# Row maxima turned by VectorE block transposes, and one PSUM bank for the projections

## The reference

```python
xq = jnp.einsum('btd,hrd->bthr', x, Q)
xk = jnp.einsum('bud,hrd->buhr', x, K)
scores = jnp.einsum('bthr,buhr->bthu', xq, xk) / sqrt(dim)
attn = jax.nn.softmax(scores, axis=3)
return jnp.einsum('bthu,bud,hde->bte', attn, x, VO)
```

```python
x = x + 0.5 * _L0_ffn_ref(_layernorm(x, axis=-1), ...)
x = x + _L0_attn_ref(_layernorm(x, axis=-1), ...)
x = x + 0.5 * _L0_ffn_ref(_layernorm(x, axis=-1), ...)
```

## Time and profile before

| | us |
|---|---|
| median of 3 runs | 1075.48 |
| the 3 runs | 1075.07 to 1076.77 |
| the profiled execution, its own time | 1076.03 |
| its span in the trace | 1074.2 |

### The profile page before, as it was taken

One profiled execution on the slowest core, in us unless ns is written; L12 is line 12 of the kernel. 1 busy time (PEld: TensorE's weight loads), 2 busy tenths in 40 slices (PEclk: granted clock), 3 DMA queues, 4 the chain that ended last, 5 costly groups with the idle time before them and its releaser, 6 DMA issues.

```text
span 1074.2 us, 21731 instructions
## 1 busy us (share of the span) xinstructions
PE 989.8 (92%) x6145; PEld 514.2 (48%) x6145; DVE 802.9 (75%) x1335; ACT 802.0 (75%) x1294; POOL 785.2 (73%) x707
## 2 busy tenths in 40 slices
PE   4758569999999999999999999999999999996897
PEld 3646324444444444444444444444444444444664
DVE  7545897777777777777777777777777777778455
ACT  4638368888887788887788888778888778885763
POOL 2624338888888888888888888888888888894442
PEclk9879889999999999999999999999999999998899
DMA  9000021222222222222222222222222222210002
GB/s 233 1 1 1 19 70 46 66 64 61 59 59 59 59 59 59 62 63 64 62 63 64 61 59 59 59 59 59 59 62 63 64 63 62 65 34 1 1 1 79
DMA packets 71675, 59.02 MB, mean 55 GB/s; under 512 B 11168, under 2 KB 70560, under 8 KB 71648
## 3 DMA queue, kind: packets, MB, share of 16 engines
q1 hardware_dynamic: 71392, 58.31, 22.1%
q10 hardware_dynamic: 256, 0.39, 0.1%
HBM read 6.23 MB, written 2.10 MB: 8 GB/s over the span
## 4 chain that ended last, share of the span: by engine, by line
PE 76%; DVE 13%; POOL 6%; issue 4%; ACT 1%; DMA 1%; SPq 0%; DVEq 0%; POOLq 0%; ACTq 0%
PE ps L995 11%; PE ps L996 10%; PE ps L997 10%; PE ps L985 10%; PE ps L986 10%; PE ps L972 6%; PE ps L1008 3%; PE ps L964 3%; PE ps L1007 3%; PE ps L1009 3%; DVE work_b L701 3%; PE ps L966 2%; PE ps L965 2%; DVE hT L708 2%; POOL u_u L332 1%
## 5 line engine op out<-in xcount | busy, mean ns | idle before, releaser
L373 POOL TENSOR_TENSOR p_lo<-work_b,p_hi 128x1024 f16<-128x1024 f32 x256 | 539.6, 2129 | 148.1 <-ACT p_hi L525 148.1
L779 DVE TENSOR_REDUCE mcol<-ps 128x2 f16<-128x1024 f32 x256 | 301.7, 1223 | 41.1 <-PE ps L972 41.0
L520 ACT ACTIVATE work_b<-ps,exp_scale 128x1024 f32<-128x1024 f32 x256 | 271.4, 1111 | 38.6 <-PE ps L986 38.4
L525 ACT ACTIVATE p_hi<-work_b 128x1024 f16<-128x1024 f32 x256 | 256.0, 1054 | 0.0
L985 PE MATMUL ps<-head_ops 128*128 128x512 f16 x512 | 195.0, 381 | 3.8 <-DVE mcol L779 2.4
L995 PE MATMUL ps<-p_hi,xn_hi 128*128 128x512 f16 x512 | 195.7, 382 | 0.0
L986 PE MATMUL ps<-head_ops 128*128 128x512 f16 x512 | 195.1, 381 | 0.0
L996 PE MATMUL ps<-p_hi,xn_lo 128*128 128x512 f16 x512 | 195.0, 381 | 0.0
L997 PE MATMUL ps<-p_lo,xn_hi 128*128 128x512 f16 x512 | 194.8, 380 | 0.0
L379 POOL TENSOR_TENSOR x<-x,o_sb 128x512 f32 (+1 forms) x128 | 162.8, 1272 | 10.6 <-DVE o_sb L798 10.6
L530 ACT ACTIVATE y_hi<-ps 128x512 f16<-128x512 f32 x128 | 76.4, 597 | 117.0 <-PE ps L997 116.8
(11 more groups left out here) (113 smaller groups left out, 1412.0 us busy)
## 6 DMA issues: line engine op xcount, KB each, us to landing
head_ops<-pair_ops SPq DMA_DIRECT2D x512, 64.0 KB, 2.0
head_ops<-pair_ops SPq DMA_DIRECT2D x128, 128.0 KB, 2.4
x<-x_dram SPq DMA_DIRECT2D x8, 256.0 KB, 6.1
out<-x SPq DMA_DIRECT2D x8, 256.0 KB, 3.0
vo_last<-wvo_dram SPq DMA_DIRECT2D x1, 1024.0 KB, 13.2
qk<-wq_dram SPq DMA_DIRECT2D x1, 512.0 KB, 5.4
qk<-wk_dram SPq DMA_DIRECT2D x1, 512.0 KB, 6.2
scl<-scales_dram ACTq DMA_DIRECT2D x8, 48.0 KB, 5.4
```

The lines of the kernel that those rows point to most:

```text
L373: pool.tensor_tensor(p_lo[:, par, rows, :], p32[:, par, rows, :], p_hi[:, par, rows, :], ALU.subtract).then_inc(plo_done, 1)
L520: nc.scalar.activation(p32[:, par, 2 * a:2 * a + 2, :], s_ps[a], ACT.Exp, scale=exp_scale[:, 0:1]).then_inc(exp_done, 1)
L525: nc.scalar.activation(p_hi[:, par, 2 * a:2 * a + 2, :], p32[:, par, 2 * a:2 * a + 2, :], ACT.Copy).then_inc(phi_done, 1)
L779: nc.vector.tensor_reduce(mcol[:, par, t, M_ROWS], s_ps[t % 2], AX.X, ALU.max, negate=True).then_inc(max_red, 1)
```

## The change

The turn of the maxima leaves TensorE. `mcol` becomes 32 columns wide for each of two heads and four tiles, the reduction writes column 0 of each 32-wide block, and VectorE turns the blocks of 32x32 itself, with four transposes of 32 partitions each, straight into `q2`. `turn_max`, its identity and its semaphore go.

Keys and queries of a pair are projected in two different slots, keys in the even slot six ahead and queries in the odd slot five ahead, both into bank 5. `q_low` and `k_low` are put behind `y_low` in VectorE's order. The written-out slots begin at -6 instead of -5. `outputs` now waits for the high half of y before its first two matmuls and for the low half before the third.

```diff
-        mcol = sb("mcol", [128, 2, TT, 128], F16)
-        M_ROWS = slice(R, R + 64, 32)
+        mcol = sb("mcol", [128, 2, 2, TT, 32], F16)
+        M_ROW = slice(R, R + 32)
...
-        qj_ps = ps[:, 5, :]
-        kj_ps = ps[:, 7, :]
+        pj_ps = ps[:, 5, :]
...
-            pool.memset(head_ops[64:65, 0:RING:2, 3, :], 1.0).then_inc(prep_p, 1)
-            pool.memset(head_ops[96:97, 1:RING:2, 3, :], 1.0).then_inc(prep_p, 1)
+            pool.memset(head_ops[64:65, 0:2, 3, :], 1.0).then_inc(prep_p, 1)
+            pool.memset(head_ops[64:65, 2:RING, 3, :], 1.0).then_inc(prep_p, 1)
...
(ScalarE's slot)
-                if j % 2 == 1 and hi + 5 < NH:
-                    ...
-                    q_high(pair, ((j + 5) // 2) % 2)
-                    k_high(pair, ((j + 5) // 2) % 2)
+                ahead = 6 - j % 2
+                if hi + ahead < NH:
+                    pair = 2 * turn + (j + ahead) // 2
+                    if lo + ahead >= 4:
+                        pair_free(pair, ((j + ahead) // 2) % 2, turn + (j + ahead) // 4)
+                    if j % 2 == 0:
+                        k_high(pair, ((j + ahead) // 2) % 2)
+                    else:
+                        q_high(pair, ((j + ahead) // 2) % 2)
...
(VectorE)
-                nc.vector.tensor_reduce(mcol[:, par, t, M_ROWS], s_ps[t % 2], AX.X, ALU.max,
+                nc.vector.tensor_reduce(mcol[:, par, :, t, 0], s_ps[t % 2], AX.X, ALU.max,
                                         negate=True).then_inc(max_red, 1)
 
-            def row_max(pair, ring):
-                dve.wait_ge(m_turned, pair + 1)
-                rows = qj_ps[64:128, :].rearrange("p (a t) -> p a t", a=1).to_broadcast([64, 2, T])
-                nc.vector.tensor_copy(q2[64:128, ring:ring + 2, :], rows).then_inc(m_ready, 1)
+            def row_max(mine, k, pair, par, ring):
+                if not isinstance(k, int) or k >= 2:
+                    dve.wait_ge(s_done, 2 * k)
+                dve.wait_ge(max_red, 4 * pair + 4)
+                for q in range(4):
+                    rows = q2[M_ROW, ring:ring + 2, :].rearrange("p a (t c) -> p a t c", c=128)
+                    ins = nc.vector.transpose(rows[:, :, :, 32 * q:32 * q + 32], mcol[32 * q:32 * q + 32, par, :, :, :])
+                ins.then_inc(m_ready, 1)
...
(TensorE)
-                if j % 2 == 0 and lo >= -2 and hi + 2 < NH:
-                    pe.wait_ge(max_red, 2 * k + 8)
-                    pe.wait_ge(ql_ready, projected(i, j))
-                    turn_max(k + 2, (j // 2 + 1) % 2)
                 if lo >= 1:
-                    pe.wait_ge(yl_ready, k)
+                    pe.wait_ge(yh_ready, k)
                     if lo >= 2:
                         pe.wait_ge(o_scaled, k - 1)
-                    pe.wait_ge(kl_ready, projected(i, j))
...
+                    if t == 0:
+                        pe.wait_ge(yl_ready, k)
                     ins = nc.tensor.matmul(o, y_lo[:, cols], vh, start=False, stop=True)
...
-                    project(qj_ps, 0, pj_head * R, quads // QPB, q_proj)
-                    if lo >= 1:
-                        pe.wait_ge(o_scaled, k)
-                    project(kj_ps, 1, pj_head * R, quads // QPB, k_proj)
+                    if j % 2 == 0:
+                        if lo >= -4:
+                            pe.wait_ge(ql_ready, pair)
+                        project(pj_ps, 1, pj_head * R, quads // QPB, k_proj)
+                    else:
+                        pe.wait_ge(kl_ready, pair + 1)
+                        project(pj_ps, 0, pj_head * R, quads // QPB, q_proj)
```

More of the change, by code:

```diff
@@ L314, in _ @@
             pool.memset(xn_lo[:, :, D - 1:D], 0.0).then_inc(prep_p, 1)
-            pool.memset(mcol[:, :, :, :], 0.0).then_inc(prep_p, 1)
+            pool.memset(mcol[:, :, :, :, :], 0.0).then_inc(prep_p, 1)
             pool.wait_ge(prep_p, 4)
@@ L415, in _ @@
             act.wait_ge(consts, 2)
-            nc.scalar.activation(ident_b[:, :], ident[:, :], ACT.Copy)
-            nc.scalar.activation(ident16[:, :], ident[:, :], ACT.Copy).then_inc(prep_a, 1)
+            nc.scalar.activation(ident_b[:, :], ident[:, :], ACT.Copy).then_inc(prep_a, 1)
             def pre(f, s):
@@ L511, in q_high @@
                 act.wait_ge(q_proj, pair + 1)
-                nc.scalar.activation(pair_ops[:, buf, 0, :], qj_ps, ACT.Copy).then_inc(qh_ready, 1)
+                nc.scalar.activation(pair_ops[:, buf, 0, :], pj_ps, ACT.Copy).then_inc(qh_ready, 1)
             def k_high(pair, buf):
                 act.wait_ge(k_proj, pair + 1)
-                nc.scalar.activation(pair_ops[:, buf, 2, :], kj_ps, ACT.Copy).then_inc(kh_ready, 1)
+                nc.scalar.activation(pair_ops[:, buf, 2, :], pj_ps, ACT.Copy).then_inc(kh_ready, 1)
             def exps(k, par, a):
@@ L550, in slot @@
                     p_high(k + 1, (j + 1) % 2, 1)
-                if j % 2 == 1 and hi + 5 < NH:
[L552 to L555, removed]
-                    q_high(pair, ((j + 5) // 2) % 2)
-                    k_high(pair, ((j + 5) // 2) % 2)
+                turn = k // 4 if quad[0] is None else quad[0]
+                ahead = 6 - j % 2
[7 more added lines that the diff above has]
+                        q_high(pair, ((j + ahead) // 2) % 2)
                 if 0 <= lo < SG:
@@ L565, in _ @@
             quad = [None]
-            for k in range(-5, 4):
+            for k in range(-6, 4):
                 slot(k, k % 4, k, k)
@@ L802, in slot @@
                 if j % 2 == 0 and lo >= -2 and hi + 2 < NH:
-                    row_max(2 * i + (j // 2 + 1), (j + 2) % 4)
+                    row_max(mine, k, 2 * i + (j // 2 + 1), (j // 2 + 1) % 2, (j + 2) % 4)
                 if lo >= 1 and lo - 1 < NH:
@@ L810, in slot @@
                         reduce_max(2 * k + (8 + a), (j // 2) % 2, 2 * (j % 2) + a)
[L811 to L818, removed]
                 if 0 <= lo < SG:
@@ L822, in slot @@
                     y_low(k)
-            for k in range(-5, 4):
+                ahead = 6 - j % 2
+                if hi + ahead < NH:
+                    pair = 2 * i + (j + ahead) // 2
+                    buf = ((j + ahead) // 2) % 2
+                    if lo + ahead >= 4:
+                        dve.wait_ge(spread_done[buf][0], 80 * (i + (j + ahead) // 4))
+                        dve.wait_ge(spread_done[buf][1], 80 * (i + (j + ahead) // 4))
+                    if j % 2 == 0:
+                        k_low(pair, buf)
+                    else:
+                        q_low(pair, buf)
+            for k in range(-6, 4):
                 slot(link, k // 4, k, k % 4, k, k)
@@ L974, in maxima @@
                 ins.then_inc(max_mm, 1)
[L976 to L980, removed]
             def scores(k, ring, a):
@@ L999, in weigh, with outputs @@
                     ins.then_inc(av_half, 1)
-            def outputs(head):
+            def outputs(k, head):
                 vh = vo_hi[:, bass.ds(head, 1), 0:RW].rearrange("p a d -> p (a d)")
@@ L1027, in slot @@
                         scores(k + 1, (j + 1) % 4, a)
-                if j % 2 == 0 and lo >= -2 and hi + 2 < NH:
-                    pe.wait_ge(max_red, 2 * k + 8)
-                    pe.wait_ge(ql_ready, projected(i, j))
-                    turn_max(k + 2, (j // 2 + 1) % 2)
                 if lo >= 1:
-                    pe.wait_ge(yl_ready, k)
+                    pe.wait_ge(yh_ready, k)
                     if lo >= 2:
                         pe.wait_ge(o_scaled, k - 1)
-                    pe.wait_ge(kl_ready, projected(i, j))
                     if hi < SG:
                         pe.wait_ge(xsplit_done, SG + k)
-                    outputs((4 * i + (j - 1)) % H)
+                    outputs(k, (4 * i + (j - 1)) % H)
                 if 0 <= lo < NH:
@@ L1056, in slot @@
                     weigh(j % 2, 1, i // QPB)
[L1057 to L1064, removed]
-                    project(qj_ps, 0, pj_head * R, quads // QPB, q_proj)
-                    if lo >= 1:
-                        pe.wait_ge(o_scaled, k)
-                    project(kj_ps, 1, pj_head * R, quads // QPB, k_proj)
+                ahead = 6 - j % 2
+                if hi + ahead < NH:
+                    pair = 2 * i + (j + ahead) // 2
+                    quads = i + (j + ahead) // 4
+                    pj_head = (quads % QPB) * 4 + (j + ahead) % 4
+                    if j % 2 == 0:
+                        if lo >= -4:
+                            pe.wait_ge(ql_ready, pair)
+                        project(pj_ps, 1, pj_head * R, quads // QPB, k_proj)
+                    else:
+                        pe.wait_ge(kl_ready, pair + 1)
+                        project(pj_ps, 0, pj_head * R, quads // QPB, q_proj)
                 if 0 <= lo < SG:
```

7 lines of the change are left out of this document (2 added, 5 removed).

## The result

The changed kernel takes 1069.2 us (median of 11 runs, 1067.2 to 1072.9), against 1075.95 for the kernel before in the same comparison: a ratio of 0.9936 (0.992 to 0.9951). The forecast was 1073.1. The profiled execution took 1072.72 us with a span of 1070.9, so it lies 3.5 above its own median.

A forecast was written before the change was run, and what follows sets the result against it. TensorE was taken as the bound, at 12.93 us a pair of slots. 1076.0 - 4.9 (steady pairs) + 2.0 (start) + 0.5 (end) = 1073.6 for the profiled execution, so 1073.1 for the median, range 1056 to 1087.

The forecast's parts named there:

- The mechanism of the slots: Steady slots: TensorE loses turns and output stall, VectorE's longer chain delays later scores; pair 12.85 us instead of 12.93.
- the sign: Whole kernel: faster by over 0.2%, chance 0.48, against 0.18 for the same and 0.34 for slower.
- the stall at the outputs: TensorE in front of the output matmuls, waiting for y's low half: about 0.11 us a pair.
- one new stall: Third pair of scores after the even slot waits for VectorE's second reduction: 0.17 and 0.26 us, 0.23 on average with restart.
- 0.47 for each, 1.88 for four: VectorE's transposes in the even slot: 0.44 us each plus a start 0.03 after the last one's end.
- I take 0.09 of the 0.11 as gone: Stall before the outputs: the split wait removes 0.09 us a pair, leaving 0.02 inside the outputs.
- The gain of the steady part: Steady slots: 61 pairs, each 0.08 us shorter, gain 4.9 us.
- I take 2.0: Start of the kernel: later query projection and longer transposes delay the first scores, costing 2.0 us, from 0.5 to 4.
- a bound for the transposes: VectorE's SBUF-to-SBUF operation, 0.27 us with GpSimd idle and 0.60 beside its subtractions, bounds a transpose from above.
- 5.65 us slots meet the same 7.33, ... 0.5: Last slots, without projections: one stall of about 0.8 us, less two turns' 0.22, costs 0.5 us.
- The order in one bank adds waits ... both are covered: Projections sharing a bank wait for q_low or k_low, done 2.18 or about 2.3 us in, needed at 4.35: no cost.
- The rival that GpSimd holds up the transposes: Even slot: first transpose waits 0.45 us for add_out, 27 us in all, 1101; chance of a step above 0.50: 0.15.

The follow-up runs named there:

- e1: The changed kernel with q_low put back in front of y_low in odd slots: 1058.47 us, ratio 0.9829 to the kernel before.
- e4: The changed kernel with all four transposes reading partitions 0 to 31 of the column of maxima: 1060.61 us, ratio 0.9841 to the kernel before.
- e11: The kernel before with only the wait of the outputs split, high half first, low half before the third matmul: 1068.71 us, ratio 0.9926.
- the first trace: Profiled execution of the changed kernel in its first comparison: 1072.72 us, span 1070.9; the second trace is that of e10.
- e10: The changed kernel run again unaltered, for a second profile: 1068.39 us, ratio 0.9926 to the kernel before, profiled execution 1068.96.
- e3: The kernel before with only the maxima turned by VectorE's transposes, projections and output wait as before: 1076.72 us, ratio 0.9998.

## Why the prediction was right, and where it was not

**The mechanism of the slots was right, and the sign, which had got a chance of 0.48.** The two costs of before, turns and the stall at the outputs, went (though the prediction saw that stall in odd slots only, and one even slot had 0.09 of it); one new stall came, at the third pair of scores of odd slots, for L778's reductions. e1 and e4 take 0.6 and 0.37 us out of the chain in front of them in two unlike ways, and both remove it.

**Step by step.** y_low ended 1.57 us after the even slot's start (1.59 forecast), a transpose took 0.437 (0.44), the reciprocal started at 4.02 (4.09), the reductions ended at 7.20 (7.26). The stalls were 0.12 and 0.21 (0.17 and 0.26), the pair 12.74 (12.85).

**Two terms were mis-sized.** "0.47 for each, 1.88 for four": measured 0.450 from start to start and 1.79 to 1.81 for four. The hold was there (e4), but the next transpose starts 0.014 after the end of the last one, not 0.03 as the reciprocal behind the cast. With it the stalls came to 0.17 a pair instead of 0.23. "I take 0.09 of the 0.11 as gone": e11 measures 0.126 for that edit alone, so nothing is left inside the outputs, and the stall of before was larger than I counted. TensorE alone needs 12.573 (e1) and not 12.62, another 0.05. The gain of the steady part was 61 x 0.19 = 11.6 us instead of 4.9.

**"I take 2.0" at the start was too small for these executions**, and it took back part of what the slots gave beyond the forecast: 3.4 in one trace and 8.0 in the other. That the sum came within 4 us of the measured time is in part luck: the two errors have opposite signs. The first scores were forecast at 145, by the chain from k_low over the query projection; they came at 146.74 and 147.65. The next rows are the first projection of before (its high halves were done at 129.50), then first projection and high half of the queries in the first trace, then both and the first scores in the second:

```profile
127.41 0.38 PE L964 MATMUL ps<-xt_hi,w_hi 128*128 128x512 f16 x1 [1.95 <-DVE xt_lo L722]
```

```profile
128.31 0.57 PE L971 MATMUL ps<-xt_hi,w_hi 128*128 128x512 f16 x1 [1.94 <-DVE xt_lo L721]
...
132.65 0.60 ACT L508 ACTIVATE pair_ops<-ps 128x512 f16<-128x512 f32 x1 [2.28 <-PE ps L973]
```

```profile
128.52 0.38 PE L971 MATMUL ps<-xt_hi,w_hi 128*128 128x512 f16 x1 [1.96 <-DVE xt_lo L721]
...
131.74 0.60 ACT L508 ACTIVATE pair_ops<-ps 128x512 f16<-128x512 f32 x1 [1.78 <-PE ps L973]
...
146.74 0.59 PE L986 MATMUL ps<-head_ops 128*128 128x512 f16 x1 [1.71 <-DVE mcol L778]
```

The steps that I had forecast are near: from the high halves to the first scores it is 0.7 us more than before in both traces (0.65 forecast), and from the first projection to the high halves 1.7 more in the second (1.7 forecast) and 2.8 in the first. What I hadn't counted is that the first projection itself comes 0.9 and 1.1 us later, ahead of all that the change moves. Over the traces of all the runs here it starts between 126.8 and 128.7, in e11, which leaves the start as it was, at 127.56; what sets it is not shown. The 1.1 by which the two traces differ goes with the clock. Three windows of 11 us that hold these steps, of before, the first trace and the second, have the granted clock as the number ahead of DMA:

```profile
127.00:138.00 11.00, 4.24 (x20) 1.35 (x20) 10.93 (x42) 3.67 (x5) 2.23 (x3) 0.97 0.35 85
```

```profile
128.00:139.00 11.00, 7.93 (x20) 1.49 (x20) 8.26 (x20) 2.10 (x4) 1.89 (x2) 0.53 0.20 48
```

```profile
128.00:139.00 11.00, 6.73 (x20) 1.37 (x20) 9.28 (x24) 2.39 (x4) 2.53 (x3) 0.66 0.22 55
```

The granted clock was 0.97 before (2.4 GHz nearly throughout), 0.53 in the changed kernel (1.2 GHz in most of the window) and 0.66 in e10, with the same 20 matmuls, which keep TensorE busy for 7.93 and 6.73 us instead of 4.24. The remainder in the slower trace is L656 behind GpSimd: from the first scores to the eleventh slot it takes 73.3 us, the other 69.6 and before 69.7. I had used that row only as a bound for the transposes, and not asked what happens to L656 itself when its moment moves. I had also read it as 0.60 us for each of four; one by one they are 1609, 334, 333 and 332 ns, so that one is held and three are not.

**The other steps.** "5.65 us slots meet the same 7.33, ... 0.5" at the end (0.8 less 0.22 is nearer to 0.6): the last slots took less instead, 41.3 against 41.7 up to the last scores and 19.4 against 20.6 from there to the last output matmul. No run takes this term apart. "The order in one bank adds waits ... both are covered" held: no projection waits in the steady slots. The rival that GpSimd holds up the transposes is out: they take 436 ns beside add_out and 440 without it. What I didn't see is that the turns covered y's low half in even slots (e3), so that the worth of an edit hung on another. By the ratios, the turns alone give nothing, the split 8 us, together 8.5, and with the moved projections and q_low in front (e1) 18.4.

## What to carry to other kernels

Work taken off the bounding engine pays only up to the next signal that arrives behind it; add up that engine's distance to the next two or three waits before counting the gain, and test the parts in pairs, since one may be another's cover. When a step moves between slots, ask what the secondary engine does in the slot that gets it, and put each cheap conversion where that engine waits anyway (here one reordering was worth 10 us, more than the whole change). The start of a kernel has to be summed like the steady part: operations that meet a shared resource there can cost several of the us that were won.

## What was unexpected of the hardware

A held instruction doesn't always pay the same: from one transpose to the next of another input group 0.014 us pass between end and start, from q_low to the first transpose and from the last to the reciprocal 0.031. With one input group for all four (e4) they overlap by 0.07.

GpSimd's fp32 subtractions of 2.1 us hold up some VectorE operations and not others in the same kernel. An fp32 tensor-scalar from SBUF to SBUF was held for the whole of a subtraction, 2141 to 2204 ns in place of 334, and which of the four were hit differed between two executions of one kernel; fp16 transposes from SBUF to SBUF (436 ns beside these subtractions in e1) and reads from PSUM with one operand in SBUF (0.69 us) were not. The Trainium skill (SBUF — State Buffer, section "Who interferes with whom") lists tensor-scalar operations among those that can take the shared port pair, which agrees, and says nothing of transposes.

The clock granted to TensorE ahead of the first scores differed between two executions of the same kernel, 0.53 and 0.66, for the same matmuls.
